# Moving k into its stacks through DRAM instead of between SBUF tiles, with a new order on every engine

## Chip, cores and metric

One core of a Trainium2 chip runs the whole program. The metric is the device time of one execution in microseconds. The kernel before took 1820.44 us, the median of three runs (1819.01 to 1821.09). A difference of 0.2% is 3.6 us.

## What is computed

A cross-attention encoder layer over 128 sequences of 128 tokens with 256 features, 16 heads of 16 features, in fp32:

```python
q = query @ Wq + bq          # split into 16 heads of 16
k = key @ Wk + bk            # key and values are ctx_1024
v = values @ Wv + bv
scores = einsum('bhqd,bhkd->bhqk', q, k) / sqrt(16)
scores = where(j < i, scores, -1e30)          # strictly causal
attn = softmax(scores); attn[:, :, 0, :] = 0
x = layer_norm(query + (attn @ v) @ Wo + bo)
out = layer_norm(x + relu(x @ W1 + b1) @ W2 + b2)   # W1: 256 x 1024
```

## The kernel before, in words

The batch is cut into 64 groups of 2 sequences (256 tokens). All engine programs are written out by hand: each has a function `iteration(it)`, called for `it` from -3 to 68, which works on several groups at once (a software pipeline). In iteration `it` TensorE computes the scores of group `it`, the k projection of group `it + 1`, the q projection and x transposes of group `it + 2`, and the feed-forward pieces of groups `it - 2` and `it - 3`. The order within an iteration is fixed by the list in the source, on each engine by itself, and semaphores join them. Nothing reorders at run time: an instruction that waits holds up all that stands behind it on its engine.

Precision is kept by splitting fp32 operands in a high and a low part (fp32r). A dense product is three matmuls (high x high, high x low, low x high) for each of two 128-row slices; a piece of 12 matmuls is a "product" below. There are 12 products in an iteration: q, k, v, the output projection (`out_project`), four of `ff_up`, four of `ff_down`. The eight score units `scores(g, 0)` to `scores(g, 7)` (L437, two matmuls each, four heads for one sequence) are the exception: there the three terms are stacked over partitions. A tile `k_stack` has 96 rows, three blocks of 32, with the high part of k, its low part and the high part again, and `q_stack` has high, high, low, so one matmul gives all three terms. [...]

- `stack_q(g, i)` (L230) issues 6 transfers, each 32 rows, for two of the four blocks `j`; 12 for a group.
- `stack_k(g, i, part)` (L246) issues transfers of 16 rows from `kT` (the projected k in SBUF, high and low) to `k_stack`. The two heads of a pair go to separate column blocks (index `e`), with zeros left in the other's rows. That makes 24 transfers for a group. `scores(g, 0)` waits for the stacks of `i = 0`, `scores(g, 1)` for those of `i = 1`.
- Besides, a group needs one load each of x (L209), c (L214) and the residual (L255), and one store (L260): 40 issues in all.

After the scores a unit goes through VectorE (`maxima` L668: mask and row maximum, in place in PSUM), ScalarE (`exponentials` L520), VectorE (`reciprocals` L662), GpSimd (`normalise` L881), TensorE (`probs_transpose` L447), ScalarE (`take_probsT` L532) and TensorE (`attend` L462). `ps_scores` has two buffers, so unit m waits for the exponentials of unit m - 2. Projections leave PSUM in two steps, high by ScalarE (`q_hi`, `k_hi` L558; `x_hi`, `c_hi`, `z_hi` L537; `h_hi` L580) and low by VectorE (`q_lo`, `k_lo` L698; `x_lo`, `c_lo`, `z_lo` L676; `take_v` L724; `h_full` L738, followed by GpSimd's `h_lo` L889). The first layer norm is `norm1_sum`, `norm1_stats`, `norm1_moments` on VectorE, `rstd1` (L904) on GpSimd, and `norm1` (L768), whose result TensorE transposes in `z_transpose` (L315). The three PSUM banks `ps_dense` are shared by twelve uses; `BANK` says which bank a use has, and `HELD_BY` which use must have been taken out before it.

Of the kernel before, what the change touches and what calls it, by code (L numbers as in the profile page):

```python
# [31 lines left out]
BANK = {"xT": 0, "zT": 1, "v": 1, "q": 1, "cT": 0, "f1_0": 1, "k": 0, "f1_1": 2, "f1_2": 1, "f1_3": 0,  # L32
        "wo": 2, "f2": 2}

HELD_BY = {"cT": ("f1_3", 4), "k": ("cT", 0), "xT": ("k", 1), "f1_3": ("xT", -4), "zT": ("q", -3),
        "f1_0": ("zT", 0), "v": ("f1_0", 2), "f1_2": ("v", -2), "q": ("f1_2", 4), "f1_1": ("f2", 1),
        "wo": ("f1_1", 1), "f2": ("wo", -1)}
# [14 lines left out]
def encoder_layer(nc, x, ctx_in, Wq, bq, Wk, bk, Wv, bv, Wo, bo, ln1_g, ln1_b, W1, b1, W2, b2, ln2_g, ln2_b, out):  # L52
    ctx = ExitStack()
    with ctx:
# [12 lines left out]
        out_v = out.rearrange("(g b) s d -> g s b d", b=GB)  # L67

# [34 lines left out]
        k_stack = [sb(f"k_stack{i}", [PARTS * 32, 4, KC, 2, GT], F32R) for i in range(2)]  # L103
# [52 lines left out]
        s_kstack = [sem(f"k_stacked{i}") for i in range(2)]  # L156
# [26 lines left out]
        def f32(ap):  # L183

            return ap.bitcast(F32)
# [19 lines left out]
        def _(sp):  # L205
# [89 lines left out]
        def _(pe):  # L295
# [130 lines left out]
            def scores(g, m):  # L426
# [3 lines left out]
                if m < 2:  # L430
                    pe.wait_ge(s_qstack[m], 16 * 2 * PARTS * (g + 1))
                    pe.wait_ge(s_kstack[m], 16 * 4 * PARTS * (g + 1))
                need(pe, s_exp, g * UNITS + m - 1)
                bank = ps_scores[m % 2]
                for i in range(2):
                    c, j = w // 2, 2 * (w % 2) + i
                    last = nc.tensor.matmul(bank[:, 2 * i:2 * i + 2, :], q_stack[g % 2][:, j, c, b * S:(b + 1) * S],  # L437
                                            k_stack[g % 2][:, j, c, :, b * S:(b + 1) * S], start=True, stop=True)
# [30 lines left out]
            def iteration(it):  # L469
                scores(it, 0)  # L470
                ff_down(it - 3, 1)
                c_transpose(it + 1)
                attend(it - 1, 3)
                z_transpose(it - 2)
                ff_down(it - 3, 2)
                probs_transpose(it - 1, 5)
                scores(it, 1)
                ff_down(it - 3, 3)
                probs_transpose(it - 1, 6)
                ff_up(it - 2, 0)  # L480
                scores(it, 2)
                k_project(it + 1)
                attend(it - 1, 5)
                probs_transpose(it - 1, 7)
                scores(it, 3)
                ff_up(it - 2, 1)
                v_project(it)
                probs_transpose(it, 0)
                scores(it, 4)
                attend(it - 1, 7)  # L490
                x_transpose(it + 2)
                probs_transpose(it, 1)
                scores(it, 5)
                ff_up(it - 2, 2)
                out_project(it - 1)
                probs_transpose(it, 2)
                scores(it, 6)
                ff_up(it - 2, 3)
                attend(it, 1)
                probs_transpose(it, 3)  # L500
                scores(it, 7)
                q_project(it + 2)
                ff_down(it - 2, 0)
                probs_transpose(it, 4)

# [5 lines left out]
        def _(act):  # L511
# [55 lines left out]
            def k_hi(g):  # L567
                if exists(g):
                    for i in range(2):
                        need(act, s_kstack[i], 16 * 4 * PARTS * g)  # L570
# [22 lines left out]
            def iteration(it):  # L593
                z_hi(it - 2)
                exponentials(it, 0)
                take_probsT(it - 1, 5)
                exponentials(it, 1)
                take_probsT(it - 1, 6)
                h_hi(it - 2, 0)
                k_hi(it + 1)  # L600
                exponentials(it, 2)
                take_probsT(it - 1, 7)
                h_hi(it - 2, 1)
                exponentials(it, 3)
                take_probsT(it, 0)
                att_hi(it - 1, 1)
                x_hi(it + 2)
                exponentials(it, 4)
                h_hi(it - 2, 2)
                take_probsT(it, 1)  # L610
                exponentials(it, 5)
                h_hi(it - 2, 3)
                take_probsT(it, 2)
                exponentials(it, 6)
                q_hi(it + 2)
                take_probsT(it, 3)
                exponentials(it, 7)
                take_probsT(it, 4)
                c_hi(it + 2)
                att_hi(it, 0)  # L620

# [5 lines left out]
        def _(dve):  # L627
# [189 lines left out]
            def iteration(it):  # L817
                q_lo(it + 1)
                norm1(it - 2)
                norm2(it - 4)  # L820
                maxima(it, 0)
                c_lo(it + 1)
                reciprocals(it - 1, 7)
                z_lo(it - 2)
                att_lo(it - 1, 0)
# [160 lines left out]
```

## Time and profile before

| what | value |
|---|---|
| median of 3 runs | 1820.44 us |
| profiled execution | 1823.35 us |
| its span, first to last instruction | 1821.6 us |
| mean granted TensorE clock | 0.985 |
| TensorE matmul busy | 1740.5 us, 96% |
| weight loads | 1635.5 us, 90% |
| VectorE, ScalarE busy | 1451.6 and 1454.9 us, 80% each |
| GpSimd busy | 1346.5 us, 74% |
| DMA, SP's queue, share of 16 engines | 35.9% |

The shares say which engine is nearly full. They don't count the SP queue, which issues transfers and computes nothing. Durations of neighbouring pipelined instructions overlap, so the cost of a piece is best read as the distance from its start to the start of the next one. Idle time is listed by the instruction that ended it; "issue" means that the profile found no releaser.

### The profile page before, as it was taken

To read this page: it belongs to the slowest core of one execution; us is meant where nothing else is said; L and a number is where in the kernel's file an instruction comes from. 1 tells how busy PE (TensorE), PEld (TensorE's weight loads), DVE (VectorE), ACT (ScalarE), POOL (GpSimd) and SP (SyncE) were. 2 spreads that over 40 slices of the span, in tenths; PEclk is the share of its full clock that TensorE was granted. 3 is DMA by queue.
4 is the path that set the end of the run, shared out by engine and by line. 5 is a ranking of instruction groups with operands and counts; after the bars stand their busy time and mean duration, and the time that the engine had idled before them with its cause. 6 is when DMAs were issued, how large, how long until landed. Compare 5 with 4: busy or idle time off the path is not lost.

```text
span 1821.6 us, 55434 instructions
## 1 busy us (share of the span) xinstructions
PE 1740.5 (96%) x17184; PEld 1635.5 (90%) x17184; DVE 1451.6 (80%) x6808; ACT 1454.9 (80%) x5697; POOL 1346.5 (74%) x1230
## 2 busy tenths in 40 slices
PE   3799999999999999999999999999999999999997
PEld 3699999999999999999999999999999899998997
DVE  4668878888887888877878878878887888887885
ACT  1778888888888888888888888888888888887883
POOL 2367777777777777777777777777777777777777
PEclk7889999999999999999999999999999999999999
DMA  6333343343333343344333333334343334333320
GB/s 159 87 97 101 85 108 104 83 108 103 83 108 104 84 108 106 80 107 105 81 106 107 80 108 104 83 107 107 81 107 106 80 108 107 80 107 106 79 67 24
DMA packets 186244, 175.68 MB, mean 96 GB/s; under 512 B 43360, under 2 KB 161120, under 8 KB 185952
## 3 DMA queue, kind: packets, MB, share of 16 engines
q1 hardware_dynamic: 185952, 172.14, 35.9%
q8 instruction: 140, 2.29, 0.6%
q14 instruction: 152, 1.25, 0.2%
HBM read 54.53 MB, written 16.78 MB: 39 GB/s over the span
## 4 chain that ended last, share of the span: by engine, by line
PE 92%; SPq 4%; issue 2%; DVE 1%; POOL 1%; DMA 0%; POOLq 0%; ACT 0%; DVEq 0%
PE ps_dense L342 29%; PE ps_dense L332 29%; PE ps_probsT L447 13%; PE ps_att L462 8%; PE ps_scores L437 7%; PE ps_dense L315 6%; SPq L246 2%; SPq L230 1%; DVE probs L635 0%; POOL hT L889 0%; DMA probs<-in_L_xattn_Wq_dram 0%; DVE u L768 0%; SPq L265 0%; DMA k_stack<-kT 0%; DVE u L801 0%
## 5 line engine op out<-in xcount | busy, mean ns | idle before, releaser
L520 ACT ACTIVATE probs<-ps_scores,negmax 128x128 f32<-128x128 f32 x2048 | 725.5, 379 | 74.3 <-DVE negmax L668 74.0
L881 POOL TENSOR_TENSOR probs<-probs,recip 128x512 f32<-128x512 f32 x512 | 533.4, 1047 | 286.3 <-DVE recip L662 286.2
L668 DVE CUSTOM_DVE_ANT_0 ps_scores<-ps_scores,mask 128x128 f32<-128x128 f32 x2048 | 531.1, 320 | 144.4 <-PE ps_scores L437 144.3
L520 ACT ACTIVATION_READ_ACCUMULATOR probs<-ps_scores,negmax 128x1 f32 x2048 | 451.0, 220 | 0.0
L332 PE MATMUL ps_dense<-zT,w 128*128 128x256 f32 x3072 | 413.5, 284 | 0.5 <-DVE h_f L738 0.5
L342 PE MATMUL ps_dense<-w,hT 128*128 128x256 f32 x3072 | 410.9, 283 | 0.4 <-POOL hT L889 0.4
L889 POOL TENSOR_TENSOR hT<-h_f,hT 128x512 fp32r<-128x512 f32 x256 | 330.0, 1289 | 91.2 <-DVE h_f L738 83.2
L332 PEld LDWEIGHTS ps_dense<-zT,w 128*128 128x128 f32 x3072 | 384.4, 189 | 0.9 <-issue 0.9
L342 PEld LDWEIGHTS ps_dense<-w,hT 128*128 128x128 f32 x3072 | 381.0, 188 | 0.6 <-issue 0.6
L447 PE MATMUL ps_probsT<-ident,probs 128*128 128x128 f32 x2048 | 316.4, 277 | 0.1
L532 ACT ACTIVATE probsT<-ps_probsT 128x508 f32<-128x508 f32 x512 | 312.3, 610 | 2.9 <-PE ps_probsT L447 2.9
L437 PE MATMUL ps_scores<-k_stack,q_stack 96*128 96x256 f32 x1024 | 243.5, 320 | 51.6 <-issue 32.6
L668 DVE DVE_READ_ACCUMULATOR2_ANT negmax<- 128x1 f32 x2048 | 285.7, 140 | 0.0
L580 ACT ACTIVATE hT<-ps_dense,b_col 128x256 fp32r<-128x256 f32 x512 | 214.7, 471 | 80.8 <-PE ps_dense L332 70.5
L447 PEld LDWEIGHTS ps_probsT<-ident,probs 128*128 128x128 f32 x2048 | 233.6, 141 | 26.6 <-issue 26.2
L738 DVE TENSOR_SCALAR h_f<-ps_dense,b_col 128x256 f32<-128x256 f32 x512 | 220.4, 472 | 5.8 <-ACT hT L580 5.8
L437 PEld LDWEIGHTS ps_scores<-k_stack,q_stack 96*128 96x128 f32 x1024 | 156.2, 192 | 66.2 <-issue 62.6
L462 PE MATMUL ps_att<-probsT,v_sb 128*32 128x128 f32 x4096 | 166.2, 280 | 0.0
L768 DVE TENSOR_SCALAR u<-u,mv,rstd 128x256 f32<-128x256 f32 x256 | 136.0, 589 | 4.0 <-POOL rstd L923 4.0
L462 PEld LDWEIGHTS ps_att<-probsT,v_sb 128*32 128x32 f32 x4096 | 96.9, 109 | 36.6 <-issue 10.9
L929 POOL TENSOR_TENSOR o_tok<-u,g_row 128x512 f32<-128x512 f32 x64 | 82.0, 1281 | 55.0 <-DVE u L768 55.0
L332 PE MATMUL ps_dense<-xT,wq 128*128 128x256 f32 x768 | 102.5, 284 | 12.1 <-DVE xT L676 12.1
(74 smaller groups left out, 2287.8 us busy)
## 6 DMA issues: line engine op xcount, KB each, us to landing
q_stack<-qT SPq DMA_DIRECT2D x768, 64.0 KB, 2.4
k_stack<-kT SPq DMA_DIRECT2D x1536, 32.0 KB, 2.0
x_tok<-in_x_dram SPq DMA_DIRECT2D x64, 256.0 KB, 3.0
c_tok<-in_ctx_dram SPq DMA_DIRECT2D x64, 256.0 KB, 3.1
x_res<-in_x_dram SPq DMA_DIRECT2D x64, 256.0 KB, 4.7
out_dram<-o_tok SPq DMA_DIRECT2D x64, 256.0 KB, 2.3
probsT<-in_L_xattn_W_dram SPq DMA_DIRECT2D x1, 1024.0 KB, 8.5
u<-in_L_xattn_W_dram SPq DMA_DIRECT2D x2, 256.0 KB, 2.9
```

What stands on the lines that cost most here:

```text
L332: last = nc.tensor.matmul(ps_dense[BANK[name]][:, i * GT:(i + 1) * GT], w[:, a, kc, ch * P:(ch + 1) * P], acts[:, c, kc, :], start=(n == 0 ...
L342: last = nc.tensor.matmul(ps_dense[BANK[name]][:, b * D:(b + 1) * D], acts[:, a, kc, b * S:(b + 1) * S], w[:, c, kc, :], start=(starts and ...
L437: last = nc.tensor.matmul(bank[:, 2 * i:2 * i + 2, :], q_stack[g % 2][:, j, c, b * S:(b + 1) * S], k_stack[g % 2][:, j, c, :, b * S:(b + 1 ...
L447: last = nc.tensor.transpose(ps_probsT[m % 2][:, i, :], probs[:, m % 4, i, :], ident[:])
L462: last = nc.tensor.matmul(ps_att[32 * j:32 * j + 32, c * S:(c + 1) * S], v_sb[g % 2][:, b, 4 * c + j, e:e + 2, :], probsT[:, unit, 2 * (j ...
L520: last = nc.scalar.activation(probs[:, m % 4, i, :], ps_scores[m % 2][:, i, :], ACT.Exp, bias=negmax[:, m % 4, i:i + 1], scale=-1.0, accum ...
L532: nc.scalar.activation(probsT[:, m % 4, :, 1:S], ps_probsT[m % 2][:, :, 1:S], ACT.Copy).then_inc(s_pTsb, 1)
L580: last = nc.scalar.activation(hT[:, 0, 2 * n + i, :], ps_dense[BANK[f"f1_{n}"]][:, i * GT:(i + 1) * GT], ACT.Relu, bias=b1_col[:, 2 * n + ...
L668: last = nc.vector.tensor_tensor_reduce(ps_scores[m % 2][:, i, :], ps_scores[m % 2][:, i, :], mask[:], -1.0, -MASKED, ALU.add, ALU.min, ac ...
L738: last = nc.vector.tensor_scalar(h_f32[:, n % 2, i, :], ps_dense[BANK[f"f1_{n}"]][:, i * GT:(i + 1) * GT], b1_col[:, 2 * n + i:2 * n + i + ...
L881: nc.gpsimd.tensor_tensor(probs[:, m % 4], probs[:, m % 4], recip[:, m % 4, :].unsqueeze(2).broadcast_to([P, 4, S]), ALU.mult)\
L889: nc.gpsimd.tensor_tensor(hT[:, 1, 2 * n:2 * n + 2, :], h_f32[:, n % 2], f32(hT[:, 0, 2 * n:2 * n + 2, :]), ALU.subtract).then_inc(s_hlo[n ...
```

## The change

k now goes through a DRAM tensor `k_spill` with two slots. `spill_k(g, part)` writes the high or the low half of `kT` with one transfer of 128 rows. `stack_k(g, part)` waits until that has landed and then reads it back with transfers of 16 rows that hold all eight (chunk, block) pairs at once: four for the high half (two blocks of the stack, two heads), two for the low. `scores(g, 0)` and `scores(g, 1)` both wait for all six. The orders on all five engines are laid out anew, and with them the bank table.

```diff
-BANK = {"xT": 0, "zT": 1, "v": 1, "q": 1, "cT": 0, "f1_0": 1, "k": 0, "f1_1": 2, "f1_2": 1, "f1_3": 0,
-        "wo": 2, "f2": 2}
+BANK = {"xT": 2, "zT": 0, "v": 1, "q": 0, "cT": 1, "f1_0": 1, "k": 0, "f1_1": 2, "f1_2": 1, "f1_3": 0,
+        "wo": 1, "f2": 2}
...
+        k_dram = nc.dram_tensor("k_spill", (2, 2, KC, P, GT), F32).ap()
+        k_rows = k_dram.rearrange("n h c (j e d) t -> n h e d (c j) t", j=4, e=2)
...
-        k_stack = [sb(f"k_stack{i}", [PARTS * 32, 4, KC, 2, GT], F32R) for i in range(2)]
+        k_stack = [sb(f"k_stack{i}", [PARTS * 32, 4 * KC, 2, GT], F32R) for i in range(2)]
...
-            def stack_k(g, i, part):
+            def spill_k(g, part):
                 if exists(g):
                     if part == 0:
                         sp.wait_ge(s_hi["k"], KC * (g + 1))
                     else:
                         sp.wait_ge(taken["k"], KC * (g + 1))
+                    need(sp, s_kstack, 16 * 2 * PARTS * (g - 1))
+                    sp.dma_start(k_dram[g % 2, part].rearrange("c p t -> p c t"), f32(kT[:, part])).then_inc(s_kspill[part], 16)
+
+            def stack_k(g, part):
+                if exists(g):
+                    sp.wait_ge(s_kspill[part], 16 * (g + 1))
                     need(sp, s_scores, (g - 1) * UNITS)
...
-                            for j in (2 * i, 2 * i + 1):
-                                for e in range(2):
-                                    sp.dma_start(
-                                        f32(k_stack[g % 2][32 * s + DK * e:32 * s + DK * (e + 1), j, :, e, :]),
-                                        f32(kT[32 * j + DK * e:32 * j + DK * (e + 1), half])).then_inc(s_kstack[i], 16)
-                    if g == 0 and i == 1 and part == 1:
+                            for e in range(2):
+                                sp.dma_start(f32(k_stack[g % 2][32 * s + DK * e:32 * s + DK * (e + 1), :, e, :]),
+                                             k_rows[g % 2, part, e]).then_inc(s_kstack, 16)
+                    if g == 0 and part == 1:
                         load_weight(5)
...
             def iteration(it):
-                stack_q(it + 1, 1)
-                stack_k(it + 1, 0, 0)
-                stack_k(it + 1, 1, 1)
-                stack_k(it + 1, 0, 1)
-                stack_k(it + 1, 1, 0)
+                stack_q(it + 1, 0)
+                store(it - 4)
+                spill_k(it + 1, 1)
                 next_x(it + 3)
-                next_c(it + 3)
+                spill_k(it + 1, 0)
+                next_c(it + 2)
+                stack_k(it + 1, 1)
+                stack_k(it + 1, 0)
                 load_residual(it)
-                stack_q(it + 2, 0)
-                store(it - 3)
+                stack_q(it + 2, 1)
```

The lists on the other engines are as long as before. Two lines show the kind of edit on TensorE:

```diff
-                c_transpose(it + 1)
+                c_transpose(it + 2)
```

SP's queue, one iteration of the steady part, before. In all these rows a name stands for `destination<-source` with the shape moved:

```order
L246 DMA k_stack<-kT 16x2x256 x24
L209 DMA x_tok<-in_x_dram 128x2x256
L214 DMA c_tok<-in_ctx_dram 128x2x256
L255 DMA x_res<-in_x_dram 128x2x256
L230 DMA q_stack<-qT 32x512 x6
L260 DMA out_dram<-o_tok 128x2x256
L230 DMA q_stack<-qT 32x512 x6
```

And now:

```order
L233 DMA q_stack<-qT 32x512 x12
L267 DMA out_dram<-o_tok 128x2x256
L243 DMA k_spill<-kT 128x2x256
L212 DMA x_tok<-in_x_dram 128x2x256
L243 DMA k_spill<-kT 128x2x256
L217 DMA c_tok<-in_ctx_dram 128x2x256
L254 DMA k_stack<-k_spill 16x8x256 x6
L262 DMA x_res<-in_x_dram 128x2x256
```

There are 24 issues where 40 were, and the x load (which waits for the x transposes) and both spills now stand ahead of the stack transfers.

TensorE's queue in the changed kernel, from the k projection (`wk`) to the last piece but one before the next group's first score unit. `w` with `zT` is `ff_up`, `w` with `hT` is `ff_down`:

```order
L339 MATMUL ps_dense<-cT,wk 128x256 x12
L339 MATMUL ps_dense<-zT,w 128x256 x12
L444 MATMUL ps_scores<-k_stack,q_stack 128x256 x2
L454 MATMUL ps_probsT<-ident,probs 128x128 x4
L469 MATMUL ps_att<-probsT,v_sb 32x128 x8
L339 MATMUL ps_dense<-zT,w 128x256 x12
L444 MATMUL ps_scores<-k_stack,q_stack 128x256 x2
L322 MATMUL ps_dense<-ident,x_tok 128x128 x4
...
L349 MATMUL ps_dense<-wo,aT 128x256 x12
```

Before, a score unit stood directly ahead of the k projection and an `attend` directly behind it; now `ff_up` pieces stand on both sides, and the x transposes come two score units after it as before.

VectorE's queue in the changed kernel at the turn of an iteration, after the row maxima of unit 7, up to those of the next unit:

```order
L669 RECIPROCAL recip<-sums 128x4
L705 SCALAR_TENSOR_TENSOR qT<-ps_dense,bq_col,qT 128x256 x2
L775 TENSOR_SCALAR u<-u,mv,rstd 128x256 x2
L683 TENSOR_TENSOR cT<-ps_dense,cT 128x512
L675 ISA ps_scores,negmax<-ps_scores,mask 128x128
```

The same place before:

```order
L662 RECIPROCAL recip<-sums 128x4
L698 SCALAR_TENSOR_TENSOR qT<-ps_dense,bq_col,qT 128x256 x2
L768 TENSOR_SCALAR u<-u,mv,rstd 128x256 x4
L668 ISA ps_scores,negmax<-ps_scores,mask 128x128
```

`norm2` (two of the four `u` instructions) has gone to another place in the iteration, and `c_lo` has come in ahead of the maxima.

## Rows read from the trace of the kernel before

**Rows 1.** The page's first part: busy time, share and instructions by engine.

```profile
PE 1740.5 (96%) x17184; PEld 1635.5 (90%) x17184; DVE 1451.6 (80%) x6808; ACT 1454.9 (80%) x5697; POOL 1346.5 (74%) x1230
```

**Rows 2.** Waits: engine, line, releaser; us in total, times, longest.

```profile
PE ps_scores L437 <- issue: 32.6, 43, 3.0
PE ps_scores L437 <- DMA k_stack<-kT: 16.2, 3, 8.3
```

**Rows 3.** Timeline of SP's queue: start us, us, engine, line, what, count.

```profile
1484.27 0.58 SPq L209 DMA_DIRECT2D x_tok<-in_x_dram  x1
...
1485.98 4.46 SPq L230 DMA_DIRECT2D q_stack<-qT  x6
...
1495.20 16.55 SPq L246 DMA_DIRECT2D k_stack<-kT  x24
1511.80 0.58 SPq L209 DMA_DIRECT2D x_tok<-in_x_dram  x1
```

**Rows 4.** Timeline of TensorE, c transposes of groups 4, 5 and 63.

```profile
120.35 0.60 PE L315 MATMUL ps_dense<-ident,c_tok 128*128 128x128 f32 x4
146.96 0.60 PE L315 MATMUL ps_dense<-ident,c_tok 128*128 128x128 f32 x4
...
1729.08 0.60 PE L315 MATMUL ps_dense<-ident,c_tok 128*128 128x128 f32 x4
```

**Rows 5.** DMA issues: count, KB each, median us from issue to landing.

```profile
q_stack<-qT SPq DMA_DIRECT2D x768, 64.0 KB, 2.4
k_stack<-kT SPq DMA_DIRECT2D x1536, 32.0 KB, 2.0
x_tok<-in_x_dram SPq DMA_DIRECT2D x64, 256.0 KB, 3.0
...
out_dram<-o_tok SPq DMA_DIRECT2D x64, 256.0 KB, 2.3
```

**Rows 6.** Timeline of TensorE, first groups: the four longest waits.

```profile
40.30 0.77 PE L437 MATMUL ps_scores<-k_stack,q_stack 96*128 96x256 f32 x2 [8.34 <-DMA k_stack<-kT]
...
44.21 1.20 PE L437 MATMUL ps_scores<-k_stack,q_stack 96*128 96x256 f32 x4 [2.29 <-DMA k_stack<-kT]
...
64.20 0.56 PE L437 MATMUL ps_scores<-k_stack,q_stack 96*128 96x256 f32 x2 [2.98 <-issue]
...
89.56 0.77 PE L437 MATMUL ps_scores<-k_stack,q_stack 96*128 96x256 f32 x2 [5.57 <-DMA k_stack<-kT]
```

**Rows 7.** Timeline of TensorE, six pieces in a row of the steady part.

```profile
1482.87 0.64 PE L462 MATMUL ps_att<-probsT,v_sb 128*32 128x128 f32 x16
1483.45 0.66 PE L315 MATMUL ps_dense<-ident,u 128*128 128x128 f32 x4
1483.86 1.68 PE L342 MATMUL ps_dense<-w,hT 128*128 128x256 f32 x12
1485.37 0.60 PE L447 MATMUL ps_probsT<-ident,probs 128*128 128x128 f32 x4
1485.73 0.48 PE L437 MATMUL ps_scores<-k_stack,q_stack 96*128 96x256 f32 x2
1486.04 1.59 PE L342 MATMUL ps_dense<-w,hT 128*128 128x256 f32 x12
```

**Rows 8.** Timeline of VectorE, the same part.

```profile
1480.77 2.10 DVE L768 TENSOR_SCALAR u<-u,mv,rstd 128x256 f32<-128x256 f32 x4
...
1486.24 0.30 DVE L668 CUSTOM_DVE_ANT_0 ps_scores<-ps_scores,mask 128x128 f32<-128x128 f32 x1 [0.45 <-PE ps_scores L437]
...
1489.77 0.30 DVE L668 CUSTOM_DVE_ANT_0 ps_scores<-ps_scores,mask 128x128 f32<-128x128 f32 x1 [1.33 <-PE ps_scores L437]
...
1490.74 0.17 DVE L662 RECIPROCAL recip<-sums 128x4 f32<-128x4 f32 x1
1490.83 0.84 DVE L738 TENSOR_SCALAR h_f<-ps_dense,b_col 128x256 f32<-128x256 f32 x2
...
1492.10 0.88 DVE L698 SCALAR_TENSOR_TENSOR kT<-ps_dense,bk_col,kT 128x256 fp32r<-128x256 f32 x2 [0.43 <-ACT kT L558]
```

More of the change, by code:

```diff
@@ L30 @@
 ITERATIONS = range(-3, NG + 5)
[L32 to L37 removed]
+BANK = {"xT": 2, "zT": 0, "v": 1, "q": 0, "cT": 1, "f1_0": 1, "k": 0, "f1_1": 2, "f1_2": 1, "f1_3": 0,
+        "wo": 1, "f2": 2}
+HELD_BY = {"f1_1": ("f2", 1), "xT": ("f1_1", 4), "f2": ("xT", -4), "zT": ("q", -3), "k": ("zT", 3),
+        "f1_3": ("k", -3), "q": ("f1_3", 4), "v": ("cT", -1), "f1_0": ("v", -2), "f1_2": ("f1_0", 0),
+        "wo": ("f1_2", 1), "cT": ("wo", 3)}
 TAKES = {"q": KC, "k": KC}
@@ L155, in encoder_layer @@
         s_qstack = [sem(f"q_stacked{i}") for i in range(2)]
-        s_kstack = [sem(f"k_stacked{i}") for i in range(2)]
+        s_kspill = [sem(f"k_{half}_in_dram") for half in ("hi", "lo")]
+        s_kstack = sem("k_stacked")
         s_scores = sem("scores_ready")
@@ L431, in scores @@
                     pe.wait_ge(s_qstack[m], 16 * 2 * PARTS * (g + 1))
-                    pe.wait_ge(s_kstack[m], 16 * 4 * PARTS * (g + 1))
+                    pe.wait_ge(s_kstack, 16 * 2 * PARTS * (g + 1))
                 need(pe, s_exp, g * UNITS + m - 1)
@@ L437, in scores @@
                     last = nc.tensor.matmul(bank[:, 2 * i:2 * i + 2, :], q_stack[g % 2][:, j, c, b * S:(b + 1) * S],
-                                            k_stack[g % 2][:, j, c, :, b * S:(b + 1) * S], start=True, stop=True)
+                                            k_stack[g % 2][:, 4 * c + j, :, b * S:(b + 1) * S], start=True, stop=True)
                 last.then_inc(s_scores, 1)
@@ L568, in k_hi @@
                 if exists(g):
-                    for i in range(2):
-                        need(act, s_kstack[i], 16 * 4 * PARTS * g)
+                    for part in range(2):
+                        need(act, s_kspill[part], 16 * g)
                     projection_hi(g, "k", kT, bk_col)
@@ L817, in iteration @@
             def iteration(it):
+                norm1_moments(it - 2)
+                maxima(it - 1, 7)
+                reciprocals(it - 1, 6)
                 q_lo(it + 1)
                 norm1(it - 2)
-                norm2(it - 4)
+                c_lo(it + 1)
                 maxima(it, 0)
-                c_lo(it + 1)
                 reciprocals(it - 1, 7)
+                att_lo(it - 1, 0)
                 z_lo(it - 2)
-                att_lo(it - 1, 0)
                 maxima(it, 1)
+                reciprocals(it, 0)
+                take_v(it)
+                maxima(it, 2)
                 norm2_sum(it - 3)
-                reciprocals(it, 0)
-                maxima(it, 2)
                 reciprocals(it, 1)
+                norm2_stats(it - 3)
+                norm2_moments(it - 3)
                 h_full(it - 2, 0)
-                k_lo(it + 1)
                 maxima(it, 3)
                 reciprocals(it, 2)
-                norm2_stats(it - 3)
-                take_v(it)
+                h_full(it - 2, 1)
+                k_lo(it + 1)
                 maxima(it, 4)
                 reciprocals(it, 3)
-                h_full(it - 2, 1)
                 att_lo(it - 1, 1)
+                h_full(it - 2, 2)
+                norm2(it - 3)
                 x_lo(it + 2)
@@ L843, in iteration @@
                 reciprocals(it, 4)
-                norm2_moments(it - 3)
-                h_full(it - 2, 2)
+                h_full(it - 2, 3)
                 norm1_sum(it - 1)
@@ L849, in iteration @@
                 reciprocals(it, 5)
-                norm1_moments(it - 1)
-                h_full(it - 2, 3)
-                maxima(it, 7)
-                reciprocals(it, 6)
             for it in ITERATIONS:
@@ L936, in iteration @@
             def iteration(it):
-                h_lo(it - 3, 2)
-                normalise(it - 1, 4)
-                rstd1(it - 2)
-                h_lo(it - 3, 3)
-                rstd2(it - 4)
-                normalise(it - 1, 5)
-                normalise(it - 1, 6)
-                scale_z2(it - 4)
-                normalise(it - 1, 7)
-                offset_z2(it - 4)
                 normalise(it, 0)
+                normalise(it, 1)
                 scale_z1(it - 2)
-                offset_z1(it - 2)
-                normalise(it, 1)
+                h_lo(it - 2, 0)
                 normalise(it, 2)
-                h_lo(it - 2, 0)
-                residual(it - 1)
+                rstd2(it - 3)
                 normalise(it, 3)
                 h_lo(it - 2, 1)
+                h_lo(it - 2, 2)
+                normalise(it, 4)
+                h_lo(it - 2, 3)
+                normalise(it, 5)
+                rstd1(it - 1)
+                normalise(it, 6)
+                offset_z1(it - 2)
+                normalise(it, 7)
+                scale_z2(it - 3)
+                offset_z2(it - 3)
+                residual(it)
             for it in ITERATIONS:
```

58 lines of the change are left out of this document (29 added, 29 removed).

## Prediction

> **What bounds the kernel now.** I began with the page's first part: TensorE is busy 96% of the span, the other engines 80% or less [rows 1]. So the end is set by TensorE's work plus the time in which it stands, and this change alters no matmul. The question is how much TensorE stands, and for what.
>
> The waits view answers: 32.6 us ahead of score matmuls in 43 waits without a named releaser, and 16.2 us in 3 waits for `k_stack` [rows 2]. The first group could be anything, so I looked at the pace. An undisturbed iteration takes 146.96 - 120.35 = 26.61 us of TensorE time; from group 4 to group 63 there are 59 iterations in 1729.08 - 120.35 = 1608.73 us, 27.27 each [rows 4]. The excess is 59 x 0.66 = 38.7 us.
>
> What has a period of 27 us? SP's queue. From one x load to the next 27.53 us pass: 1.71 for three loads, 9.22 for twelve q transfers and a store, 16.60 for 24 k transfers, and the next x load follows at once [rows 3]. That is 40 issues at 0.69 us each. SP has no idle time to give; it is slower than TensorE by the same 0.7 us or so, and TensorE waits for the last k transfers whenever the lag has eaten its lead. That is why the profile names no releaser: SP's issue rate is the bound, while a single transfer needs only 2.0 us to land [rows 5]. I count the unnamed waits as waits for k for that reason.
>
> **The change, part by part.** *SP's queue.* Removed: 24 issues, 16.60 us. Added: two spills and six reads back. Total 24 issues instead of 40; at 0.69 that is 16.6 us an iteration, 10 below TensorE's 26.61. So SP's rate stops being a bound, and what was wholly its work (38.7 us) goes, provided that the new chain for k, now longer, ends in time.
>
> *The chain for k.* I place the pieces of the new TensorE list by start-to-start distances: a score unit 0.31, a transpose of probabilities 0.36, `attend` 0.58, an input transpose 0.41 [rows 7]. In an iteration stand 8, 8, 4 and 3 of them, 8.91 us, which leaves 17.70 for the 12 products, 1.475 each (the row shows 1.51 for one). Counted from `scores(it, 0)`: three score units, three probability transposes, the z transposes, one `attend` and three products come first, so the k projection starts at 7.4. `k_lo` does not follow it at once. On VectorE it stands behind `maxima(3)`, a reciprocal and `h_full(1)`. Score unit 3 starts at 10.4; its maxima start 0.51 later (1485.73 to 1486.24), take 0.97 with the way to the reciprocal, then 0.09, then 0.84 for `h_full` and 0.88 for `k_lo` [rows 7, 8]: done at 13.7. Then SP: spill low at 13.7; the x load waits for the x transposes (start 13.4, done 14.0) and goes at 14.3; spill high, c load, until 15.7. No row shows a spill; the output store, SBUF to DRAM with as many bytes and rows, lands in 2.3 [rows 5], so the low half is there at 16.0 (16.7 with the 3.0 of a load). Two low reads, then four high ones, at 0.69: the last is issued at about 19.5. Between the 2.0 of a 32 KB transfer and the 3.0 of a 256 KB load [rows 5] I take 3.0, since the source is DRAM as in the load: landed at 22.5. `scores(it + 1, 0)` is due at 26.6. Slack 4.1 us.
>
> Behind SP's wait for the spill stand the stack reads, the residual load and the q transfers. The residual waits for `norm1_sum` of the same iteration at about 20 anyway, and GpSimd needs it only in the next. The q transfers for group it + 2 wait for `q_lo` past the iteration's end, and their scores are a whole iteration off. So these waits cost nothing while the slack lasts. If it is gone, each us late is a us in every iteration.
>
> The upper bound for the reads is another reading of the rows: 64 KB to 32 rows takes 0.4 us more than 32 KB to 16 rows [rows 5]. If all bytes to few rows move at 32 KB in 0.4 us, one transfer after another, six of 128 KB need 9.6 us, and the last lands at 16.0 + 1.6 + 9.6 = 27.2, which is 0.6 late. I don't take it: the difference can also be fixed cost, and 256 KB to 128 rows costs just 1.0 us more than 32 KB. The Trainium skill has a rule that speaks for it (SBUF — State Buffer, on the DMA port swizzle): a transfer's bandwidth depends on how many of 16 ports its partitions reach. By it, 16 consecutive rows reach 4 ports, an estimated 109 GB/s of the page's 435; six reads would need 7.2 us, and the last would land near 25, still in time. No row of this case shows a transfer of 128 KB to 16 rows.
>
> *The new order.* No instruction of the compute engines is added or removed. The cost is nil if every operand is ready when TensorE comes to it. I went through the new lists with the distances above, and the tightest place is the turn of an iteration. From `scores(7)` to `z_transpose` TensorE has a score unit, the c transposes, a probability transpose, `attend`, a product, a score unit and a probability transpose: 3.8 us. In that time VectorE must do 0.51 + 0.97 + 0.09 for unit 7, then `q_lo` (0.88) and two of the four `u` instructions (half of 2.10, 1.1 with the end) [rows 8]: 3.55 us. Slack about 0.3. Placed in the same way, `take_v` behind the v projection frees the bank for `ff_up(0)` with some 0.4 to spare. The softmax has less room than before too: from `scores(7)` to the transpose of its result stood 15 us, and now 9, of which the chain through four engines uses about 6. All fit, so I set 0, with 0.3 us an iteration (18 us in 59) as the upper bound.
>
> *Start.* The four longest waits of the first groups are 8.34, 2.29, 2.98 and 5.57, 19.2 in sum [rows 6]; all are SP's 24 issues. For group 0 the new queue has spill, x load, spill, c load, the wait, two reads, four weight loads and four reads to issue, about 9 us with the landing of the spill, and 3 for the last landing. The last of the old transfers landed at 44.2; going back 2.0 for the landing, 24 issues and four loads of 0.5, SP came to k at about 24. So k is there at 36 instead of 40.3: 4.3 of the first wait goes, and the other three go whole. Together 15.2, between 7 (if the spill's round trip stays in the path of every first group) and 22 (if the smaller waits there go too). *End:* the last store and the last layer norm stay as they are; 0.
>
> **Sum:** 38.7 + 15.2 = 53.9 us. Against the profiled execution, 1823.35 - 53.9 = 1769.4; it stands 2.9 above the median of the runs, so for that I forecast 1820.44 - 53.9 = **1766.5 us**.
>
> **Rivals.** *A, small stalls of the new order* (chance 0.20). For it: slacks of 0.3 to 0.4 by distances that I read off single rows. Against: with the old order the undisturbed iterations kept 26.61 exactly. At 0.3 us in 59 iterations: 1784. *B, slow reads* (0.06): the last read lands at 27.2, every iteration is 0.6 late, the steady gain falls to 3 and the start gives 7: 1810. *C, slower than before* (0.04): at `z_transpose`, if the chain of 3.55 us above is longer, for example because `rstd1` on GpSimd, which now stands behind `normalise(5)`, comes late to `norm1`. Each 0.1 us over the slack costs 6 us. It overtakes the whole gain when the chain passes 3.8 + 53.9/59 = 4.7 us; at 5.0 the time would be 1766.5 + 59 x 1.2 = 1837. Against it: `rstd1` has nearly 3 us between `moments` and its use. *D, nothing happens* (0.02): the unnamed waits are not for k. Then 32.6 stays, and with some gain at the start and loss elsewhere it is 1820. Against it: the excess over 26.61 and SP's excess agree.
>
> **How the numbers follow.** Forecast 0.68, A 0.20, B 0.06, C 0.04, D 0.02. The forecast's own range is 1757 to 1777 by the bounds of the start; A reaches up to 1790. I give 1755 to 1790, which leaves out B, C, D and the edges. A measurement can tell 0.2%, 3.6 us, from nothing. Faster: forecast, A and most of B, 0.93; the same 0.02; slower 0.05.
>
> **What would show it.** In the profile after: SP's list with 24 issues in 17 us and then idle; c transposes 26.6 us apart from group 4 to 63; no unnamed waits ahead of score matmuls; reads of k landing in 2.5 to 3.3 us; first scores near 36 us. I am wrong if the iteration is not 26.6: a wait ahead of `z_transpose` or the first `ff_up` means A or C, one ahead of `scores(0)` with late landings means B.

## The result, and the profile after

The changed kernel takes 1836.86 us (median of 4 runs, 1834.3 to 1838.34), where the kernel before, run again beside it, took 1820.69. The ratio is 1.0089 with a 95% interval of 1.0072 to 1.0107. It is slower by 0.9%; the forecast was 1766.5 us, the range 1755 to 1790.

The profile has a span of 1836.5 us. First the queue that the change was made for: SP, the queue of SyncE, which issues all the transfers. Its timeline in the changed kernel, one iteration (start us, us, engine, line, what, count):

```profile
1493.22 8.22 SPq L233 DMA_DIRECT2D q_stack<-qT  x12
1501.49 0.58 SPq L267 DMA_DIRECT2D out_dram<-o_tok  x1
1507.90 0.36 SPq L243 DMA_DIRECT2D k_spill<-kT  x1
1508.49 0.37 SPq L212 DMA_DIRECT2D x_tok<-in_x_dram  x1
1508.96 0.43 SPq L243 DMA_DIRECT2D k_spill<-kT  x1
1509.44 0.47 SPq L217 DMA_DIRECT2D c_tok<-in_ctx_dram  x1
1510.65 4.52 SPq L254 DMA_DIRECT2D k_stack<-k_spill  x6
1516.02 0.39 SPq L262 DMA_DIRECT2D x_res<-in_x_dram  x1
```

This is as forecast: 24 issues. The rows add up to 15.3 us of an iteration's 27.6, so SP stands for the rest. The waits for k in the steady part, which [rows 2] showed, are gone. But TensorE isn't quicker. Its timeline, c transposes of groups 4, 5 and 63, to be set beside [rows 4]:

```profile
111.63 0.60 PE L322 MATMUL ps_dense<-ident,c_tok 128*128 128x128 f32 x4
139.24 0.60 PE L322 MATMUL ps_dense<-ident,c_tok 128*128 128x128 f32 x4
...
1739.40 0.60 PE L322 MATMUL ps_dense<-ident,c_tok 128*128 128x128 f32 x4
```

59 iterations in 1627.77 us are 27.59 each, against 27.27 before and 26.61 for an undisturbed one. And they are all alike: 27.56 to 27.61 in the steady part, where before they lay between 26.6 and 29.6. So nothing falls behind any more as SP did; something costs the same in every iteration. The page's first part, its chain of work that ended last, and one group of the view by line (line, engine, operation, shapes, count | busy us, mean ns | idle before) say which engine to look at:

```profile
PE 1771.2 (96%) x17184; PEld 1647.6 (90%) x17184; DVE 1653.7 (90%) x6808; ACT 1438.3 (78%) x5697; POOL 1350.2 (74%) x1230
...
PE 64%; DVE 31%; issue 2%; POOL 1%; DMA 1%; ACT 0%; SPq 0%; POOLq 0%; DVEq 0%; ACTq 0%
...
L775 DVE TENSOR_SCALAR u<-u,mv,rstd 128x256 f32<-128x256 f32 x256 | 294.1, 1188 | 1.6 <-POOL rstd L930 0.8 <-POOL rstd L911 0.8
```

VectorE (DVE in the profile) is busy 202 us more than before with the same 6808 instructions [rows 1], and has 31% of the chain that ended last, where it had 1% before. Its layer norm instruction, `u` in place, takes 1188 ns on average. By line, VectorE in the kernel before, the same instruction and three others:

```profile
L738 DVE TENSOR_SCALAR h_f<-ps_dense,b_col 128x256 f32<-128x256 f32 x512 | 220.4, 472 | 5.8 <-ACT hT L580 5.8
L768 DVE TENSOR_SCALAR u<-u,mv,rstd 128x256 f32<-128x256 f32 x256 | 136.0, 589 | 4.0 <-POOL rstd L923 4.0
L754 DVE BATCH_NORM_STATS2 stats<-u 128x6 f32<-128x256 f32 x256 | 93.9, 408 | 0.1
...
L762 DVE TENSOR_SCALAR var_eps<-mv 128x2 f32<-128x2 f32 x128 | 24.2, 189 | 4.4
```

And in the changed kernel:

```profile
L745 DVE TENSOR_SCALAR h_f<-ps_dense,b_col 128x256 f32<-128x256 f32 x512 | 219.8, 471 | 10.8 <-ACT hT L587 7.3
L761 DVE BATCH_NORM_STATS2 stats<-u 128x6 f32<-128x256 f32 x256 | 96.0, 416 | 0.1
L769 DVE TENSOR_SCALAR var_eps<-mv 128x2 f32<-128x2 f32 x128 | 93.6, 732 | 4.4
```

Two instructions grew, and both are `tensor_scalar` from SBUF to SBUF. `var_eps` works on two columns, and the same instruction took 169 ns at the median before, so most of its 732 ns isn't work. The same operation with its source in PSUM (`h_f`) and `bn_stats`, which only reads SBUF, kept their times: no `h_f` took more than 488 ns, and 374 of the 512 ran wholly inside a GpSimd instruction. What is beside the long ones? VectorE, then GpSimd (POOL in the profile), at the place where the norm has 2.79 us for two instructions:

```profile
1509.42 0.86 DVE L745 TENSOR_SCALAR h_f<-ps_dense,b_col 128x256 f32<-128x256 f32 x2
1510.20 2.79 DVE L775 TENSOR_SCALAR u<-u,mv,rstd 128x256 f32<-128x256 f32 x2
1512.92 0.68 DVE L683 TENSOR_TENSOR xT<-ps_dense,xT 128x512 fp32r<-128x512 f32 x1
```

```profile
1509.27 1.04 POOL L888 TENSOR_TENSOR probs<-probs,recip 128x512 f32<-128x512 f32 x1 [1.17 <-DVE recip L669]
1510.27 2.57 POOL L896 TENSOR_TENSOR hT<-h_f,hT 128x512 fp32r<-128x512 f32 x2
```

GpSimd runs two `h_lo` back to back until 1512.84; the norm's two instructions, one for each, end at 1512.99, 0.15 us behind it. That lag holds throughout: each of the 188 norm instructions of this trace that take over 0.6 us ends 0.14 to 0.16 us after a GpSimd instruction. `x_lo` stands behind them, and TensorE's `ff_down(0)` needs the bank that `x_lo` frees:

```profile
1513.03 0.40 PE L444 MATMUL ps_scores<-k_stack,q_stack 96*128 96x256 f32 x2
1513.65 0.63 PE L349 MATMUL ps_dense<-w,hT 128*128 128x256 f32 x3 [0.22 <-DVE xT L683]
```

From the score unit to `ff_down(0)` it is 0.61 us at the median over the steady part. The same happens ahead of `z_transpose` (`norm1` beside `normalise(6)` and `offset_z1`): 0.65 us from the probability transposes to it, where a product follows them at 0.36, and they follow other transposes at 0.44:

```profile
1025.38 0.60 PE L454 MATMUL ps_probsT<-ident,probs 128*128 128x128 f32 x4
1026.03 0.44 PE L322 MATMUL ps_dense<-ident,u 128*128 128x128 f32 x2
```

### The profile page after: what moved, and what is told of

The parts are those of the page before. It is cut to its first block, busy times and chain, and to the rows that moved or that the text cites. A ratio compares the mean times of both kernels' runs of the same rounds, so it can differ in the third digit from the quotient of the medians.

```text
span 1836.5 us, 54408 instructions
## 1 busy us (share of the span) xinstructions
PE 1771.2 (96%) x17184; PEld 1647.6 (90%) x17184; DVE 1653.7 (90%) x6808; ACT 1438.3 (78%) x5697; POOL 1350.2 (74%) x1230
## 4 chain that ended last, share of the span: by engine, by line
PE 64%; DVE 31%; issue 2%; POOL 1%; DMA 1%; ACT 0%; SPq 0%; POOLq 0%; DVEq 0%; ACTq 0%
PE ps_dense L339 25%; PE ps_dense L349 21%; DVE u L775 14%; PE ps_probsT L454 6%; DVE ps_scores L675 5%; PE ps_scores L444 5%; PE ps_att L469 4%; DVE h_f L745 3%; PE ps_dense L322 3%; DVE qT L705 2%; DVE xT L683 2%; DVE negmax L675 2%; DVE aT L753 1%; POOL hT L896 1%; DVE probs L642 0%
## 5 line engine op out<-in xcount | busy, mean ns | idle before, releaser
L349 PE MATMUL ps_dense<-w,hT 128*128 128x256 f32 x3072 | 424.3, 288 | 13.8 <-DVE xT L683 12.7
L527 ACT ACTIVATION_READ_ACCUMULATOR probs<-ps_scores,negmax 128x1 f32 x2048 | 433.9, 212 | 0.0
L339 PE MATMUL ps_dense<-zT,w 128*128 128x256 f32 x3072 | 422.0, 287 | 0.5 <-DVE h_f L745 0.5
L349 PEld LDWEIGHTS ps_dense<-w,hT 128*128 128x128 f32 x3072 | 381.0, 188 | 38.7 <-DVE xT L683 24.9
L339 PEld LDWEIGHTS ps_dense<-zT,w 128*128 128x128 f32 x3072 | 379.2, 189 | 13.5 <-issue 13.2
L454 PE MATMUL ps_probsT<-ident,probs 128*128 128x128 f32 x2048 | 309.6, 274 | 0.0
L775 DVE TENSOR_SCALAR u<-u,mv,rstd 128x256 f32<-128x256 f32 x256 | 294.1, 1188 | 1.6 <-POOL rstd L930 0.8
L454 PEld LDWEIGHTS ps_probsT<-ident,probs 128*128 128x128 f32 x2048 | 239.4, 141 | 0.2 <-issue 0.2
L745 DVE TENSOR_SCALAR h_f<-ps_dense,b_col 128x256 f32<-128x256 f32 x512 | 219.8, 471 | 10.8 <-ACT hT L587 7.3
L444 PE MATMUL ps_scores<-k_stack,q_stack 96*128 96x256 f32 x1024 | 215.5, 292 | 13.8 <-DMA q_stack<-qT 6.8
L339 PE MATMUL ps_dense<-xT,wq 128*128 128x256 f32 x768 | 107.7, 291 | 11.7 <-DVE xT L683 11.7
L349 PE MATMUL ps_dense<-wv,cT 128*128 128x256 f32 x768 | 109.6, 293 | 0.0
```

Of the source, the lines that this page charges most:

```text
L339: last = nc.tensor.matmul(ps_dense[BANK[name]][:, i * GT:(i + 1) * GT], w[:, a, kc, ch * P:(ch + 1) * P], acts[:, c, kc, :], start=(n == 0 ...
L349: last = nc.tensor.matmul(ps_dense[BANK[name]][:, b * D:(b + 1) * D], acts[:, a, kc, b * S:(b + 1) * S], w[:, c, kc, :], start=(starts and ...
L454: last = nc.tensor.transpose(ps_probsT[m % 2][:, i, :], probs[:, m % 4, i, :], ident[:])
L527: last = nc.scalar.activation(probs[:, m % 4, i, :], ps_scores[m % 2][:, i, :], ACT.Exp, bias=negmax[:, m % 4, i:i + 1], scale=-1.0, accum ...
L745: last = nc.vector.tensor_scalar(h_f32[:, n % 2, i, :], ps_dense[BANK[f"f1_{n}"]][:, i * GT:(i + 1) * GT], b1_col[:, 2 * n + i:2 * n + i + ...
L775: nc.vector.tensor_scalar(u[:, b, :], u[:, b, :], mv[:, n, b, 0:1], rstd[:, n, b:b + 1], ALU.subtract, ALU.mult).then_inc(s_z, 1)
```

## The experiments

Three theories. **L**: VectorE's SBUF-to-SBUF `tensor_scalar` does not run beside a GpSimd instruction, and the new orders put them side by side. **M**: the DRAM route's traffic slows VectorE's SBUF instructions. **O**: the new sequence of pieces costs TensorE time by itself. An iteration below is the distance from the c transposes of group 4 to those of group 63, divided by 59. Each time is a median of at least four executions, but r2's, which is one; each ratio is to the kernel before on the same chip. Different runs stand on different chips, where the kernel before took 1821 to 1828 us, so runs are best compared by ratio or by iteration.

### Each half of the change alone

**r1_old_orders_dram_route** puts the spills and reads into the kernel before and keeps all its orders and banks:

```diff
             def iteration(it):
                 stack_q(it + 1, 1)
-                stack_k(it + 1, 0, 0)
-                stack_k(it + 1, 1, 1)
-                stack_k(it + 1, 0, 1)
-                stack_k(it + 1, 1, 0)
+                spill_k(it + 1, 0)
+                spill_k(it + 1, 1)
+                stack_k(it + 1, 0)
+                stack_k(it + 1, 1)
                 next_x(it + 3)
```

> The orders of the kernel before on every engine, with only k's way changed (two spills, six reads). Theory L (the layer norm's in-place VectorE instruction doesn't run beside a GpSimd instruction, and the new orders put them side by side): the norm instruction stays at its 589 ns mean, an iteration takes 26.6 us, no waits for k: 1765 to 1780 us. Rival M (the DRAM route's traffic slows VectorE's SBUF instructions): the norm instruction's mean rises towards 1188 ns and an iteration takes 27 us or more: 1800 to 1840 us.

Measured: 1767.71 us, ratio 0.9682 (0.9652 to 0.9713). Line by line, VectorE of this run, and the c transposes of groups 4 and 63:

```profile
L775 DVE TENSOR_SCALAR u<-u,mv,rstd 128x256 f32<-128x256 f32 x256 | 135.9, 589 | 4.0 <-POOL rstd L930 4.0
```

```profile
105.19 0.60 PE L322 MATMUL ps_dense<-ident,c_tok 128*128 128x128 f32 x4
...
1675.37 0.60 PE L322 MATMUL ps_dense<-ident,c_tok 128*128 128x128 f32 x4
```

That is 26.61 an iteration. The norm instruction is as long as before to the nanosecond with all the DRAM traffic beside it, so M falls. The DRAM route is worth 3.2%, and the new orders take away more than that.

**r2_new_orders_sbuf_route** is the other half: the new orders with `stack_k(it + 1, 0, 0)`, `(1, 1)`, `(0, 1)`, `(1, 0)` in place of the spills and reads.

> The new orders with the old 24 transfers between SBUF tiles, in their old sequence, between the store and the x load. Theory L: the norm instruction's mean stays near 1188 ns though nothing goes through DRAM; k arrives late (k_lo ends about 14 us into the iteration and 24 issues and a landing take 18.6), so the time is 1880 us or more. Rival M: the mean falls to 400 to 600 ns.

Measured: 2308.7 us. The norm instruction's mean is 1179 ns with nothing going through DRAM. The size of the time has another cause than I expected; the waits view, TensorE:

```profile
PE ps_dense L315 <- DMA c_tok<-in_ctx_dram: 374.7, 63, 13.2
```

The new orders want c a whole iteration earlier, and its load stands behind 24 transfers of k. An iteration takes 35.1 us instead of 27.6. These orders need a short SP queue; here the old route isn't merely late, it holds up the loads. Not all of the extra time is theirs: TensorE, which stands more, was granted a mean clock of 0.90 here against 0.99, and its busy time rose from 1771 to 1884 us.

### Taking the two instructions apart

**r3_x_lo_first** and **r4_offset_moved** each move one instruction of the changed kernel:

```diff
-                norm2(it - 3)
                 x_lo(it + 2)
+                norm2(it - 3)
                 maxima(it, 5)
```

> The changed kernel with norm2 and x_lo swapped on VectorE, so that x_lo no longer stands behind two norm instructions that take 1.3 us each. Theory L: the 0.3 to 0.4 us wait ahead of ff_down(0) goes, 0.35 x 60 = 20 us: 1816 us; the norm2 instructions still take 1.3 us each, since both stand beside two h_lo of GpSimd. Rival O (the loss is in TensorE's new sequence of pieces, not in a wait): no change beyond 3 us.

```diff
                 h_lo(it - 2, 2)
+                offset_z1(it - 2)
                 normalise(it, 4)
                 h_lo(it - 2, 3)
                 normalise(it, 5)
                 rstd1(it - 1)
                 normalise(it, 6)
-                offset_z1(it - 2)
```

> The changed kernel with GpSimd's offset_z1 moved from behind normalise(6) to behind h_lo(2), away from norm1 on VectorE. Theory L: norm1's two instructions take 1.2 us or less instead of 1.9 and the 0.2 us wait ahead of z_transpose goes: 1824 us, and the norm instruction's mean falls to 950 to 1050 ns. Rival M: norm1's instructions keep their length and the time stays at 1837.

Measured: r3 1805.34 us, ratio 0.9893 (0.9860 to 0.9926), 27.07 an iteration; r4 1819.77 us, ratio 0.9955 (0.9935 to 0.9974), 27.30 an iteration. So the place behind `norm2` was worth 0.52 us an iteration, more than the 0.35 I expected (r3 came 11 us below its forecast), and the one behind `norm1` 0.29 (4 us below). The distances on TensorE say where: in r3 the one from the score unit to `ff_down(0)` falls from 0.61 to 0.24 us, and that product then takes 1.42 instead of 1.53; in r4 the one to `z_transpose` falls from 0.65 to 0.44. In r3 the norm's mean is 1050 ns, since `norm2`'s pair fell from 2.79 to 2.19 us, where I had expected it to stay. In r4 it is 957 ns and `var_eps` fell from 732 to 532, though no VectorE instruction was touched: the length follows what GpSimd does beside it.

**r5_both_moves** has both:

> The changed kernel with both moves: x_lo ahead of norm2 on VectorE, offset_z1 behind h_lo(2) on GpSimd. Theory L: neither the wait ahead of ff_down(0) nor that ahead of z_transpose is left; an iteration goes from 27.60 to 26.9 us (the one of x_lo first took 27.11), 1792 us. If the two waits hide one another, no better than the 1805 of x_lo first alone.

Measured: 1790.29 us, ratio 0.9802 (0.9772 to 0.9831), 26.81 an iteration, the norm at 823 ns. The two gains add up (0.52 + 0.29 = 0.81, measured 0.78), and both distances are the short ones (0.24 and 0.44).

**r10_short_h_lo** changes no order at all. It cuts two of GpSimd's instructions short, which leaves out 248 of 256 columns of the low part in two of the four h pieces:

```diff
+                    cols = 8 if g > 0 and n in (1, 2) else GT
-                    nc.gpsimd.tensor_tensor(hT[:, 1, 2 * n:2 * n + 2, :], h_f32[:, n % 2],
+                    nc.gpsimd.tensor_tensor(hT[:, 1, 2 * n:2 * n + 2, 0:cols], h_f32[:, n % 2, :, 0:cols],
...
```

> The changed kernel with GpSimd's h_lo(1) and h_lo(2) cut to 8 of 256 columns a slice from the second group on (the rest of those low parts stays as group 0 left it, so 2 of the 4 low h parts are stale). Nothing is changed on VectorE. Theory L (VectorE's norm instruction waits for the GpSimd instruction beside it): norm2's two instructions, 1.3 us each beside those two h_lo, take about 0.4 each; the mean of all falls from 1188 to about 700 ns, the wait ahead of ff_down(0) goes as in r3_x_lo_first, 27.1 us an iteration, 1803 to 1810 us. Rival M: norm2's instructions keep 1.3 us and the time is 1837.

Measured: 1802.2 us, ratio 0.9869 (0.9835 to 0.9903), 27.07 an iteration, as in r3. VectorE by line, then its timeline and GpSimd's at the same place:

```profile
L775 DVE TENSOR_SCALAR u<-u,mv,rstd 128x256 f32<-128x256 f32 x256 | 167.9, 695 | 1.6 <-POOL rstd L931 0.8 <-POOL rstd L912 0.8
```

```profile
1020.80 0.76 DVE L775 TENSOR_SCALAR u<-u,mv,rstd 128x256 f32<-128x256 f32 x2
```

```profile
1020.87 0.45 POOL L897 TENSOR_TENSOR hT<-h_f,hT 128x16 fp32r<-128x16 f32 x2
```

GpSimd's pair went from 2.57 to 0.45 us, and VectorE's, which has nothing to do with it in data, from 2.79 to 0.76. On TensorE `ff_down(0)` now follows its score unit at once:

```profile
1023.63 0.40 PE L444 MATMUL ps_scores<-k_stack,q_stack 96*128 96x256 f32 x2
1023.87 0.51 PE L349 MATMUL ps_dense<-w,hT 128*128 128x256 f32 x3
```

`z_transpose`, whose neighbours weren't touched, still comes after 0.65. This shows L directly: the wait is for the neighbour, and ends with it.

**r7_norm_one_port** tried a form of the norm instruction that might not wait: 255 columns written through a view of 5 by 51, and the last column by an instruction of its own.

```diff
-                    nc.vector.tensor_scalar(u[:, b, :], u[:, b, :], mv[:, n, b, 0:1], rstd[:, n, b:b + 1],
-                                            ALU.subtract, ALU.mult).then_inc(s_z, 1)
+                    for src, dst in ((u[:, b, 0:255], u[:, b, 0:255].rearrange("p (a c) -> p a c", a=5)),
+                                     (u[:, b, 255:256], u[:, b, 255:256])):
+                        last = nc.vector.tensor_scalar(dst, src, mv[:, n, b, 0:1], rstd[:, n, b:b + 1],
+                                                       ALU.subtract, ALU.mult)
+                    last.then_inc(s_z, 1)
```

> The changed kernel with all orders as they are; only the form of the norm instruction differs: 255 of the 256 columns are written through a view of 5 by 51 and read through one of 255, the last column by an instruction of its own, which keeps VectorE from its two-port fast mode. Same numbers out. Theory L: though the instruction does more cycles of work, it no longer waits for GpSimd: about 350 to 400 ns for 255 columns in place of 1188, both waits of TensorE go, an iteration of 26.9 us, 1795 us. Rival M or one of plain overload of VectorE: the instruction stays near 1.2 us or gets longer, and the time is 1837 us or more.

Measured: 1858.86 us, ratio 1.0177 (1.0147 to 1.0208). The form wasn't what I meant it to be. The profile shows the view folded back into one run:

```profile
L777 DVE TENSOR_SCALAR u<-u,mv,rstd 128x255 f32<-128x255 f32 x256 | 280.9, 1097 | 1.6 <-POOL rstd L933 0.8 <-POOL rstd L914 0.8
L777 DVE TENSOR_SCALAR u<-u,mv,rstd 128x1 f32<-128x1 f32 x256 | 66.9, 261 | 0.0
```

Rows of 51 that follow one another are one row of 255, and the instruction behaves as before: 374 ns at the least, against 379 for 256 columns, and 1492 at the most. The one-column instruction behind it is the find that I passed over. It has the same operation, operands and tiles, and it never waits: 257 to 270 ns in all 256 cases, 128 of them wholly inside a GpSimd instruction, while `var_eps` with its two columns takes up to 907 ns in the same trace. So a form that escapes the wait exists; whether there is one for 256 columns stays open. The run also shows the price of VectorE's time at these places: the distances to `z_transpose` and `ff_down(0)` grow to 0.83 and 0.80 us, and an iteration takes 27.96 instead of 27.59.

### What is left of the new orders

**r6_moves_and_pe_pairs** is r5 with four swaps on TensorE, of which two are:

```diff
-                probs_transpose(it, 2)
                 attend(it, 1)
+                probs_transpose(it, 2)
...
+                probs_transpose(it, 3)
                 ff_down(it - 2, 0)
-                probs_transpose(it, 3)
                 q_project(it + 2)
```

> r5_both_moves, and on TensorE three attends go ahead of the probability transposes that they followed, and probs_transpose(3) follows scores(6) at once. Theory O (what is left over 26.6 us is the cost of the sequence of pieces: the distance from a probability transpose to an attend is 0.53 us, to a product 0.36): 0.1 to 0.3 us an iteration less, 1775 to 1788 us. If the sequence costs nothing: the time of r5_both_moves within 3 us.

Measured: 1786.44 us, ratio 0.9778 (0.9753 to 0.9802), 26.71 an iteration: 0.10 less than r5, at the low edge of what was expected. The two intervals overlap, so only the iteration tells it; that measure is steady, since r1, r9 and r11, on two chips, agree to 0.01 us over all 59 iterations. **r8_one_port_and_pairs** put the same swaps on r7.

> r7_norm_one_port with the TensorE sequence of r6_moves_and_pe_pairs. Theories L and O together: 26.6 to 26.8 us an iteration, 1772 to 1788 us, near the 1768 of the old orders with the DRAM route. If either is wrong: that much longer.

Measured: 1856.72 us, ratio 1.0164 (1.0139 to 1.0189), 27.91 an iteration. With r7's premise gone its expectation couldn't hold. The swaps are worth 0.06 us an iteration here, where they were worth 0.10 on r5.

**r12_weights_after_reads** is r6 with `load_weight(5)` under `part == 0` instead of `part == 1`, behind all reads of k.

> r6_moves_and_pe_pairs with the four loads of W2 (1 MB) for group 0 issued behind all six reads of k instead of between the second and the third. If the late first scores of the new orders (43.7 us, against 35.6 with the old orders and the same route) come from reads queued behind that megabyte: scores(0, 0) near 38 us and 4 to 6 us won, 1781 us. If they come from elsewhere: 1786 us.

Measured: 1781.45 us, ratio 0.9773 (0.9755 to 0.9792). The first score units, r6 and then r12:

```profile
42.36 1.19 PE L444 MATMUL ps_scores<-k_stack,q_stack 96*128 96x256 f32 x4 [5.42 <-DMA k_stack<-k_spill]
```

```profile
37.93 0.71 PE L444 MATMUL ps_scores<-k_stack,q_stack 96*128 96x256 f32 x4 [1.95 <-DMA k_stack<-k_spill]
```

4.4 us earlier, and the profiled spans differ by 5.6 (1785.2 and 1779.6). In the new SP list a megabyte of W2 stood ahead of four of the first six reads. How much of the 4.4 us is W2 is less clear than this pair looks. In the eight kernels that share r6's SP list the first read is issued between 27.0 and 29.7 us and the first score unit comes between 39.0 and 43.7, and r6 is one of the late ones. What W2 does show in is the reads themselves: from the first issue to the last landing they take 8.9 us in r12 and 10.8 to 13.9 in those eight. And the times don't settle it, since r6 and r12 ran on different chips and their ratios, 0.9778 and 0.9773, are the same within the intervals.

**r9_late_memsets** looks at the same wait at the start of the program, on top of r1, with r1 repeated as **r11_dram_route_again**:

```diff
+            pool.wait_ge(s_wlo, 2)
             for tile in k_stack:
                 nc.gpsimd.memset(f32(tile[:]), 0.0).then_inc(s_kzero, 1)
```

> r1_old_orders_dram_route with GpSimd's memsets of the k stacks held until VectorE has split the first two weights. Theory L: the first VectorE instruction on SBUF (512 columns, 6.7 us, ends 0.3 us after the last memset) takes 0.8 us; the first q projection starts near 7 us instead of 12.3 and 4 to 5 us are won: 1763 us. If the memsets are not what it waits for: 1768.

> r1_old_orders_dram_route once more, on the same chip as r9_late_memsets, to compare with: 1767 to 1769 us.

Measured: r9 1766.97 us (1765.94 to 1768.51), r11 1767.17 us (1766.24 to 1768.39): no difference. VectorE's first instruction, in r11 and then in r9:

```profile
3.58 6.85 DVE L642 TENSOR_SCALAR probs<-probs 128x512 f32<-128x512 f32 x1 [3.58 <-DMA probs<-in_L_xattn_Wq_dram]
```

```profile
3.81 0.43 DVE L642 TENSOR_SCALAR probs<-probs 128x512 f32<-128x512 f32 x1 [3.81 <-DMA probs<-in_L_xattn_Wq_dram]
```

The time missed the forecast of 1763, but the wait is as theory L has it: 6.4 us of an instruction were waiting for memsets, which read nothing. The first q projection began at 7.05 instead of 12.28. But the first score unit came only 1.1 us earlier (34.49 against 35.62), since TensorE then stands 3.0 us for the second x load and 6.2 for k's reads. A stall undone where another wait ends later gives little back, and here nothing that the runs can tell.

## Why the prediction was wrong

**SP's rate as the bound: right.** Removing 16 issues freed it. In r1 the steady part takes 1675.37 - 105.19 = 1570.18 us where it took 1608.73 [rows 4]: 38.55 gained, 38.7 forecast.

**The start: right with the old orders.** Group 4 comes at 105.19 in r1 and at 120.35 before: 15.16, forecast 15.2. That it meets to 0.04 is luck: r11, the same kernel, has its group 4 at 103.82. The end gave 2.1 more, forecast 0. The whole of r1 is 1767.71, and the forecast of 1766.5 is, in effect, the time of that kernel. In the changed kernel the c transposes stand some 4.8 us earlier in the list, so its 111.63 means a start only about 4 us better. The rest went to late first scores (43.7 us where I said 36). Part of that varies with no change to SP's list, which gave 39.0 in r5, and part is W2 in the middle of the reads, 1.8 us at the least by their landing times in r12. I had counted its four issues there, and not its bytes.

**The chain for k: right in its end, wrong in one size.** A read took 4.6 us to land at the median, not the 3.0 that I took from the loads. The page's table of issues:

```profile
k_stack<-k_spill SPq DMA_DIRECT2D x384, 128.0 KB, 4.6
k_spill<-kT SPq DMA_DIRECT2D x128, 256.0 KB, 3.0
```

From the issue of the first read to the last landing the six took 9.2 us at the median, where my sum has 6.5 and my upper bound 11.2. So of the slack of 4.1 us 2.3 were left at the median and 0.8 at the least (3.7 and 1.6 in r1), and no steady wait came of it. With the port rule of the Trainium skill that I set beside it (SBUF — State Buffer, on the DMA port swizzle) the sum would have been an estimated 8.8, and the trace is near it; no run here separates ports from the common queue.

**The new order, cost 0 and at most 0.3 us an iteration: this is the step that failed.** It cost 0.98 (27.59 against 26.61), 58 us in 59 iterations. One place was the one that I had named as the tightest, `z_transpose`: from `scores(7)` to it TensorE takes 4.20 us where I had placed 3.8. The other, the bank that `x_lo` frees for `ff_down(0)`, I hadn't placed at all, and it cost more. The fault was in the durations: I took an instruction's length from a row where it had one neighbour and moved it to a place where it had another. The two `norm` instructions were 1.1 us in my sum; they take 1.9 at one place and 2.8 at the other. The trace of the kernel before already said so: four of them take 2.10 us where I read them [rows 8], but over the run their median is 403 ns, their mean 589 and the largest 1371, and 66 of the 256 end 0.15 us after a GpSimd instruction. It even had a VectorE instruction of 512 columns with 6.6 us at its start. I read neither.

The Trainium skill states a rule for this, and I did not use it. The Trainium skill's page SBUF — State Buffer (SBUF: two separate sides) says that VectorE and GpSimd share a pair of ports, that a VectorE instruction in a 2-port mode and a GpSimd instruction each take it as an exclusive lock, and that whichever starts second is blocked until the first has ended; the Trainium skill's page Advanced Engine Details and Errata (VectorE Performance Modes) lists `tensor_scalar` with source and destination in SBUF among those that use it. The runs agree in what waits (1188 ns against 471 for the PSUM source) and how long (until the neighbour ends, r10). That the port is the cause is the Trainium skill's word; r7, which was to test it, did not, though its one-column instruction shows that the wait depends on the instruction's form and not on its operation and tiles alone.

Split by the runs, of 0.98 us an iteration 0.52 stood behind `norm2` (r3), 0.29 behind `norm1` (r4), 0.78 with both moved (r5); 0.10 is TensorE's sequence of pieces (r6); the last 0.10 is not resolved. The forecast for the profiled execution was 1769.4 us and it took 1838.3: of the 68.9 between them 57.6 are this cost in the steady part, and the other 11 are the start, which gave about 4 instead of 15.2.

**The rivals.** A had the kind and a third of the size, 0.3 us an iteration against 0.98. C had one of the two places and the sign, and named a late `rstd1`, which wasn't it; I gave it 0.04. Its 1837 meets the measured 1836.86 by luck: it puts 1.2 us an iteration on `z_transpose`, where r4 found 0.29. B and D did not occur. The best kernel here is r1 (1767.71 us), the DRAM route with the orders left alone; r9 on top of it is the same within the measurement.

## What to carry to other kernels

When an order moves, an instruction's duration is not a constant that moves with it: read minimum, median and mean of it, and where they differ find out what stood beside it before and what will now. In this kernel VectorE's SBUF-to-SBUF `tensor_scalar` of two columns or more and GpSimd's instructions are to be planned as if on one engine, with what frees a bank for TensorE ahead of them, not behind. And a change in two parts is worth two runs: here one part was worth -3.2% and hid a loss of 4%.

## What was not expected of the hardware

- The wait shows as a longer instruction, not as idle time, so the waits view has nothing of VectorE waiting there and the engine looks busier: VectorE rose from 80% to 90%. Only TensorE's waits for `u` and `xT` give a hint. A two-column `var_eps` took 732 ns on average.
- GpSimd memsets, which read nothing, held a VectorE instruction for 6.4 us (r11 against r9).
- The same operation on one column instead of 255 was never held (r7).
- Reads of 128 KB into 16 rows land in 4.4 to 4.6 us at the median, 256 KB into 128 rows in 3.0 for the x loads [rows 5]. SP issues six of them in 2.7 us in r1, 0.45 each, where transfers between SBUF tiles took 0.69 [rows 3].
